# The low parts of y by accumulating DMAs within SBUF in place of subtractions on GpSimd

## The reference

```python
x_q = jnp.einsum('oc,bcn->bno', w_qk, y)
x_k = jnp.einsum('oc,bcn->bon', w_qk, x)
x_v = jnp.einsum('oc,bcn->bon', w_v, x) + b_v[None, :, None]
energy = jnp.einsum('bnc,bcm->bnm', x_q, x_k)
attention = jax.nn.softmax(energy, axis=-1)
attention = attention / (1e-07 + attention.sum(axis=1, keepdims=True))
x_r = jnp.einsum('bcn,bnm->bcm', x_v, attention)
x_r = jax.nn.relu(jnp.einsum('oc,bcn->bon', w_t, x - x_r) + b_t[None, :, None])
return x + x_r
```

## Time and profile before

| | us |
|---|---|
| median of 3 runs | 1848.16 |
| lowest and highest run | 1847.73, 1849.26 |
| span of the profiled execution, first to last instruction | 1846.8 |
| TensorE busy (PE) | 1841.7 |
| VectorE busy (DVE) | 1499.5 |
| ScalarE busy (ACT) | 1310.9 |
| GpSimd busy (POOL) | 788.0 |

### The profile page before, as it was taken

One profiled execution on the slowest core, in us unless ns is written; L12 is line 12 of the kernel. 1 busy time (PEld: TensorE's weight loads), 2 busy tenths in 40 slices (PEclk: granted clock), 3 DMA queues, 4 the chain that ended last, 5 costly groups with the idle time before them and its releaser, 6 DMA issues.

```text
span 1846.8 us, 26440 instructions
## 1 busy us (share of the span) xinstructions
PE 1841.7 (100%) x8901; PEld 1553.5 (84%) x8901; DVE 1499.5 (81%) x2034; ACT 1310.9 (71%) x1799; POOL 788.0 (43%) x422
## 2 busy tenths in 40 slices
PE   9999999999999999999999999999999999999999
PEld 8888888888888888888888888888888888888887
DVE  7878787787887877878878788787787877878777
ACT  7767776677666786667776677766677666776665
POOL 5543344432444424444244452444533444334431
PEclk9999999999999999999999999999999999999999
DMA  3201111011110111101111111111011110111101
GB/s 108 68 25 57 58 68 68 23 68 46 68 68 23 68 46 68 68 33 58 46 68 68 48 43 46 68 68 61 30 48 66 68 68 23 64 50 68 68 1 46
DMA packets 34090, 101.92 MB, mean 55 GB/s; under 512 B 4224, under 2 KB 5248, under 8 KB 34048
## 3 DMA queue, kind: packets, MB, share of 16 engines
q1 hardware_dynamic: 33760, 101.07, 15.8%
q10 hardware_dynamic: 288, 0.39, 0.1%
HBM read 67.90 MB, written 33.55 MB: 55 GB/s over the span
## 4 chain that ended last, share of the span: by engine, by line
PE 98%; DVE 1%; ACT 0%; issue 0%; POOL 0%; DVEq 0%; ACTq 0%; POOLq 0%
PE pv L796 37%; PE row_b L691 19%; PE row_a L691 14%; PE pv L768 9%; PE row_b L754 5%; PE row_a L754 5%; PE row_a L745 5%; PE row_b L745 5%; DVE colsum L536 0%; PE pv L898 0%; PE pv L754 0%; PE pv L931 0%; PE pv L902 0%; ACT p_sb L336 0%; DVE z_lo L503 0%
## 5 line engine op out<-in xcount | busy, mean ns | idle before, releaser
L218 POOL TENSOR_TENSOR y_lo<-y_raw,y_hi 128x896 fp32r<-128x896 f32 (+1 forms) x128 | 277.1, 2190 | 546.7 <-ACT y_hi L297 357.1
L543 DVE SCALAR_TENSOR_TENSOR p_lo<-p_sb,row_inv,p_hi 128x1024 fp32r<-128x1024 f32 x254 | 325.4, 1282 | 96.0 <-ACT p_hi L344 95.9
L327 ACT ACTIVATE ev<-row_b 128x512 f32<-128x512 f32 x384 | 229.5, 598 | 199.7 <-PE row_b L691 199.1
L203 POOL TENSOR_TENSOR x_lo<-x_sb,x_hi 128x1024 fp32r<-128x1024 f32 x63 | 152.2, 2415 | 449.2 <-ACT x_hi L280 449.2
L336 ACT ACTIVATE p_sb<-p_sb,neg_max 128x1024 f32<-128x1024 f32 x256 | 295.1, 1154 | 28.6 <-DVE neg_max L518 24.6
L344 ACT ACTIVATE p_hi<-p_sb,row_inv 128x1024 fp32r<-128x1024 f32 x256 | 292.4, 1143 | 30.7 <-PE pv L796 30.0
L536 DVE SCALAR_TENSOR_TENSOR colsum<-p_sb,row_inv,colsum 128x1024 f32<-128x1024 f32 x224 | 291.7, 1302 | 8.5 <-DVE row_inv L526 0.6
L796 PE MATMUL pv<-p_hi,z_hi 128*128 128x512 f32 x1024 | 273.7, 389 | 0.0
L796 PE MATMUL pv<-p_hi,z_lo 128*128 128x512 f32 x1024 | 273.7, 389 | 0.0
L518 DVE CUSTOM_DVE_ANT_0 p_sb<-row_a,ev 128x1024 f32<-128x1024 f32 x128 | 156.6, 1223 | 143.6 <-PE row_a L691 143.6
L796 PE MATMUL pv<-p_lo,z_hi 128*128 128x512 f32 (+1 forms) x1047 | 271.7, 383 | 0.0
(11 more groups left out here) (157 smaller groups left out, 3585.9 us busy)
## 6 DMA issues: line engine op xcount, KB each, us to landing
x_sb<-x SPq DMA_DIRECT2D x64, 512.0 KB, 4.6
out<-res SPq DMA_DIRECT2D x62, 512.0 KB, 3.4
y_raw<-y SPq DMA_DIRECT2D x64, 256.0 KB, 3.7
y_raw<-y SPq DMA_DIRECT2D x32, 512.0 KB, 3.7
out<-res SPq DMA_DIRECT2D x2, 256.0 KB, 2.1
res<-w_qk SPq DMA_DIRECT2D x1, 256.0 KB, 3.0
res<-w_t_T SPq DMA_DIRECT2D x1, 256.0 KB, 6.7
res<-w_v SPq DMA_DIRECT2D x1, 256.0 KB, 7.8
```

Source lines behind the costliest of these rows:

```text
L218: nc.gpsimd.tensor_tensor(y_lo[:, of:, cols], y_raw[:, 1 + of:8, cols], y_hi[:, of:, cols].bitcast(FP32), ALU.subtract).then_inc(y_lo_done, 1)
L327: nc.scalar.activation(ev[:, to, :], bank_b, ACT.Copy, scale=scale).then_inc(b_copied, 1)
L543: nc.vector.scalar_tensor_tensor(out=p_lo[r][:, :], in0=p_sb[r][:, :], scalar=row_inv[:, j:j + 1], in1=p_hi[r][:, :].bitcast(FP32), op0=AL ...
```

## The change

For every batch but the first, the subtraction y_lo = y_raw - y_hi on GpSimd is replaced. ScalarE writes y_lo = -y_hi right behind each `y_high` (it waits for its own `y_hi` first). GpSimd then issues a DMA from `y_raw` to `y_lo` that adds to what stands there, both in SBUF, 128 partitions by 7 pieces of 128 elements (512 bytes). TensorE and SyncE wait for that DMA, by one semaphore for each piece t, where they waited for the subtraction. The first batch keeps its subtractions. The programs of SyncE and GpSimd are written out for all batches where the steady ones were a loop.

```diff
             def batch(b, par, first=False, last=False):
                 if not last:
                     sp.wait_ge(y_hi_done, NP * (b + 1))
-                    sp.wait_ge(y_lo_done, NP * (b + 1))
+                    if first:
+                        sp.wait_ge(y_lo_done, NP)
+                    else:
+                        for t in range(NP):
+                            sp.wait_ge(y_lo_added[t], DMA * b)
                     load_y(b + 1)
...
+            def y_low_added(b, t):
+                pool.wait_ge(y_neg_done, NP * (b - 1) + t + 1)
+                cols = slice(t * P, (t + 1) * P)
+                pool.dma_start(y_lo[:, :, cols], y_raw[:, 1:8, cols], accum_op=ALU.add).then_inc(y_lo_added[t], DMA)
+
...
                 if not last:
                     y_sums(b + 1)
-                    y_low(b + 1, 0)
+                    y_low_added(b + 1, 0)
                     for kt in range(KT):
                         x_low(b + 1, 1 - par, kt)
                     pool.wait_ge(p_lo_done, NT * (b + 1))
                     for t in range(1, NP):
-                        y_low(b + 1, t)
+                        y_low_added(b + 1, t)
                     t_three(b + 1)
                     t_low(b + 1, 0)
                     t_low(b + 1, 1)
...
                 nc.scalar.activation(y_hi[:, of:, cols], y_raw[:, 1 + of:8, cols], ACT.Copy).then_inc(y_hi_done, 1)
+                if not first:
+                    act.wait_ge(y_hi_done, NP * b + t + 1)
+                    nc.scalar.activation(y_lo[:, :, cols], y_hi[:, :, cols].bitcast(FP32), ACT.Copy,
+                                         scale=-1.0).then_inc(y_neg_done, 1)
...
                 if first:
                     pe.wait_ge(a_lo_done, 1)
+                elif y_first:
+                    pe.wait_ge(y_lo_done, t + 1)
                 else:
-                    pe.wait_ge(y_lo_done, NP * b + t + 1)
+                    pe.wait_ge(y_lo_added[t], DMA * b)
```

More of the change, by code:

```diff
@@ L135, in xattn_kernel @@
         last_out = [sem(f"last_out{q}") for q in range(4)]
+        y_neg_done, y_lo_added = sem("y_neg_done"), [sem(f"y_lo_added{t}") for t in range(NP)]
         x_lo_done, y_lo_done = sem("x_lo_done"), sem("y_lo_done")
@@ L189, in _ @@
                 sp.dma_start(bt_sb[:, :], b_t.rearrange("(k p) -> p k", p=P)).then_inc(bias_in, DMA)
-            run_batches(sp, lambda b: batch(b, 0, first=True), lambda b: batch(b, 1), batch,
-                        lambda b: batch(b, 1, last=True))
+            for b in range(B):
+                batch(b, b % 2, first=b == 0, last=b == B - 1)
             for q, mt, cols in ((3, 1, right), (0, 0, left), (2, 1, slice(0, C))):
@@ L259, in _ @@
                                     ALU.subtract).then_inc(wtT_lo_done, 1)
-            run_batches(pool, lambda b: batch(b, 0), lambda b: batch(b, 1), batch,
-                        lambda b: batch(b, 1, last=True))
+            for b in range(B):
+                batch(b, b % 2, last=b == B - 1)
             for r in range(2):
@@ L693, in product, with p1 @@
                 return last
-            def p1(b, t, first=False):
+            def p1(b, t, first=False, y_first=False):
                 if first:
                     pe.wait_ge(a_lo_done, 1)
+                elif y_first:
+                    pe.wait_ge(y_lo_done, t + 1)
                 else:
-                    pe.wait_ge(y_lo_done, NP * b + t + 1)
+                    pe.wait_ge(y_lo_added[t], DMA * b)
                 if t == 0:
@@ L843, in next_pair @@
             def next_pair(b, t, first=False):
-                p1(b, t)
+                p1(b, t, y_first=first)
                 p5(b, t)
```

## The result

The changed kernel takes 1854.05 us (median of 6 runs, 1852.54 to 1858.86), against 1847.74 for the kernel before (6 runs): a ratio of 1.0037, with 1.0027 to 1.0047 as its 95% interval (the two medians alone give 1.0034). It is slower by 6.3 us, where the prediction said 2040, 192 us slower. The time lies in the range and the kernel is slower, as forecast, but that was luck: the size is wrong by a factor of 30, the mechanism of the forecast did not occur, and the loss came by another path. The profiled execution took 1853.51 us with a span of 1851.6.

A forecast was written before the change was run, and what follows sets the result against it. TensorE, busy 1841.7 of 1846.8 us, was taken to bound the kernel. With c = 5.0, each boundary loses 3 x 5.0 - 8.8 = 6.2 us, 192 over 31: span 2039, median 2040 us, range 1846 to 2400.

The forecast's parts named there:

- the mechanism of the forecast: GpSimd's three issues hold back t_three, so ScalarE's z_high is late and TensorE waits: 6.2 us a boundary; chance 0.50.
- the term c: Time of one DMA issue on GpSimd, three ahead of t_three: taken as 5.0 us, between 2.1 and 7.7.
- SyncE's 0.33: SyncE's issue time for a y load, 0.33 us, used as the lower bound for GpSimd's issue c.
- formula 3c - 8.8: TensorE's loss in us at each of 31 boundaries through t_three and z_high; nothing while c is under 2.93.
- Rival 1: GpSimd's DMA issue is short, c under 2.93: no change, 1848 us; chance 0.25.
- Rival 2: Short issues, slow transfers: third DMA lands after 937.5, y load and sums late, ScalarE's y_high waits; 2034 us; chance 0.10.
- The negations on ScalarE: 124 more copies on ScalarE, near 1.0 us each: no cost, with less than 0.2 us of slack left in pair 2.
- GpSimd's work can't be won: TensorE has no holes, so taking work off GpSimd can shorten the kernel by no more than some 5 us.

The follow-up runs named there:

- the version with both causes removed: Changed kernel, batch 1 subtracted on GpSimd, wait for the last p_lo before the DMAs kept only in batch 0: 1847.53 us against 1847.31, ratio 1.0002.
- the early issue: Changed kernel without GpSimd's wait for the batch's last p_lo before the DMAs of pieces 1 to 3: 1849.00 us against 1847.74, ratio 1.0007.

## Why the prediction was wrong, and where it was right

- **The step that failed is the term c**, "I take **c = 5.0**". The trace has 1.64 us for an issue that waits for nothing, and 5.08 / 3 = 1.7 in the row of three. It lies under the 2.93 at which the prediction's own formula turns to nothing lost; so `t_three` was done 1.0 us earlier and not 8.7 later. The prediction argued against SyncE's 0.33 by the number of pieces, with two steps of 2.4 ns for each. The runs show about 0.75 ns for a piece and 0.97 us for the issue, so more than half of an issue did not go by the pieces, and the rate for them was six times too high (4.8 against 0.75). The 6.3 us that were lost did not come by this term at all.
- **The formula 3c - 8.8 held.** Idle subtractions worth 4.2 us cost 1.62 to 1.72 us at a boundary (1.7 by the formula with the 10.5 us that the row took), and six issues of 7.88 us cost nothing on that chain.
- **Rival 1 had the right condition and the wrong consequence.** c is under 2.93, but "no change" followed only if nothing else moved. The time, 6.3 us over, is closest to this case. Where the prediction says that TensorE waited 1.1 us at the very start "and nothing after it", that is so of its matmuls; its weight loads waited three times more, about 0.5 us each, for ScalarE's copies in the first batch. It was there that the negations cost something.
- **Rival 2 had the right first link.** The third DMA landed late: SyncE's load, which waits for it, went out at 932.81 on the clock of before. That is inside the 937.5 that the rival asked for, so ScalarE's `y_high` never waited. But between "early enough for `y_high`" and "harmless" lay something that the prediction had not asked: what VectorE does at the time at which the sums now run. In the kernel before, the last sum ended at 936.7 and VectorE's first column sum started at 941.22. These 4.5 us were the real slack of the sums, which now start 6.05 us later (937.60 against 931.55). The transfers themselves were priced too high, at 7.7 us each: the new queue's packets took 28.3% of 16 x 1851.6 us over 113088, 0.074 us each and not 0.138. The loads' packets, from which the 0.138 came, hold 3.0 KB on average and these 0.5.
- **The negations on ScalarE were right in the steady batches.** In the pair 2 that answers to the earlier trace rows the first copy starts at 900.39 - 3.48 = 896.91, as before, and TensorE waits for no copy there. The prediction had allowed 0.2 us of delay there. Only the first batch, which has two copies and two negations close together, was missed: a weight load waits 1.3 us and TensorE stands idle for 0.9 of it, 0.7 to 0.8 in the medians.
- **"GpSimd's work can't be won" was right.** Even the version with both causes removed equals the kernel before, since TensorE had next to no holes to fill.
- **The sum**: 6.3 us = 5.0 for the late sums (the early issue took them away) + 0.7 to 0.8 for the first batch + 0.5 that is under the noise of these comparisons. The first two are differences of medians; one profiled execution can split them otherwise, as the changed kernel's does (1.78 and 3.2).

Why some batches of the changed kernel lose 0.8 us and others nothing, its trace answers. Counted from `z_high`, the column sum starts at 10.91 to 10.97 us in each of the 30 batches, and the first sum at 7.31 to 8.45. In 29 of the 30 the column sum ends 0.54 to 0.56 us after the third sum ends, and once 0.60, so the later that sum, the longer it takes. The eight batches that lose time are the eight in which it takes 1.19 us or more; up to 1.13 it costs at most 0.10. What stays open is what moves the sums: SyncE's loads go out at 2.53 to 3.06 us, and the first sum follows 4.76 to 5.65 us behind, so most of the scatter lies in the loads of y and only some in the accumulating DMAs.

## What to carry to other kernels

Follow what a transfer's landing releases, and not only when its first reader needs it: here it held the reload of the buffer, the reload held GpSimd's sums, and the sums met VectorE. Before work on GpSimd moves in time, look in VectorE's timeline for what it will lie beside; here a column sum of 0.75 us became 1.87 and an accumulation of 1.29 became 2.41. And where the profile shows TensorE busy all the time, as here, an offload of another engine has next to nothing to gain and only slack to spend.

## What the runs showed of the hardware

- **GpSimd's DMA issue**: 1.64 us for 896 pieces, whether they have 512 or 1536 bytes, and 2.61 for the same pieces in two issues; by the line through these, about 0.97 us plus 0.75 ns for each piece. A tensor operation right behind issues has a longer record (`t_three` 1.54 us behind three and 4.32 behind six, instead of 1.28), but it begins before the last issue's record ends, and ends 1.3 us after it: `t_three` is no slower.
- **The accumulating transfer within SBUF**: 448 KB land 6.0 to 6.1 us after the issue (medians) where the DMAs are apart and 8.1 us (median of all four of a batch) where three go in a row. They move at 145 GB/s in pieces of 512 bytes and at 187 in pieces of 1536. The Trainium skill (DMA: Bandwidth & Descriptors, section "Anatomy of one DMA — SWDGE (gpsimd) path") gives 2.0 us plus the bytes at 436 GB/s, by which 3.1 us would be the estimate here, with generation "small, variable". The trace doesn't agree on the landing, which takes twice that. The issue's 1.64 us is the smaller part of the 6.0, but over a quarter of it.
- **VectorE beside GpSimd**: the tensor_scalar with one input in SBUF ends some 0.55 us after GpSimd's operation that is under way when it starts (0.75 becomes up to 1.87), and that operation keeps its 1.30. GpSimd's next one, which starts while the tensor_scalar still runs, takes 1.63 instead of 1.30. In the run with one DMA for three pieces a column sum that started 0.07 us ahead of a sum kept its 0.75, and the sum took 1.83. With two inputs in SBUF both slow down (VectorE 1.29 to 2.41, GpSimd 1.29 to 2.3). With one input in SBUF and one in PSUM VectorE stays at 1.27. The Trainium skill (SBUF — State Buffer, section "Who interferes with whom") says that VectorE in a mode with two ports and GpSimd lock each other out of a shared pair for a whole instruction, that two inputs in SBUF contend with GpSimd's reads, and that one such input in an ordinary mode does not. The traces agree on the last two, and on the first if the column sum runs in such a mode: it is a tensor_scalar, which the section counts among the operations that can, and takes 0.75 us where others of its size take 1.28, but no view shows the mode.
